# Row maxima of the second query tile in one instruction over two PSUM banks, with the order tables planned anew

## The chip, the cores and the metric

The kernel runs on one core of a Trainium2 chip. A core has five engines that run in parallel, each through its own in-order queue: TensorE (PE) for matmuls into PSUM, VectorE (DVE), ScalarE (ACT), GpSimd (POOL), and SyncE (SP), which issues most DMAs. The metric is the device time of one execution in microseconds (us); lower is better.

## The reference

Two layers run on `x` of 8 x 256 x 128. What the change touches is the attention of layer 0: 16 heads of width 8, once with ordinary queries and keys and once with six-component "lines" made from exterior products. Both softmaxes are causal.

```python
qkv = (x @ qkv_w + qkv_b).reshape(B, T, 3, H, dh)
std_logits = jnp.einsum('bhqd,bhkd->bhqk', q, k) * scale
w1 = (x_prev @ w1_write).reshape(B, T, H, 4)
write_lines = exterior(w1, w2)
read_lines = exterior(r1, r2)
J_write = jnp.einsum('bthi,ij->bthj', write_lines, _J6)
...
combined = (1.0 - gate) * std_out + gate * geo_out
return combined @ out_w + out_b
```

Around it stand, each with a residual and a layer norm: a feed-forward block with blockwise FP4 quantisation (layer 0), a Mamba block with a state scan over 256 steps, and a feed-forward block whose weights get a small data-dependent part ("LoRA", layer 1):

```python
x = _layernorm(x + _L0_attn_ref(...))
x = _layernorm(x + _L0_ffn_ref(x, w_gate, w_up, w_down))
x = _layernorm(x + _L1_attn_ref(...))   # the Mamba block
x = _layernorm(x + _L1_ffn_ref(...))    # the LoRA block
```

## The kernel before

**Turns.** The eight batch elements go through a software pipeline. Turn `k` (from -2 to 8) does `prep` for element k+2 (projections, splitting of the attention operands into bf16 parts), `core` for k+1 (logits, maxima, exponentials, weighting of the values), `norm`, `ffn`, `mamba` and `scan` for k, and `mamba_out` and `lora_ffn` for k-1. A turn has a front part (the chain norm, ffn, mamba of element k, with `prep`, the LoRA block and the first half of `core` between) and a scan part (the Mamba scan on DVE, with the second half of `core` on PE and ACT between).

**What sets the order.** Each engine's program is written out by `interleave`, which merges the streams of a turn by due times. The tables `PLAN` (turns 1 to 6) and `EDGE` (turns -1, 0, 7, 8) give one due time for each step of each stream (a step ends at a `yield`). The numbers are only an order: whatever stands earlier in an engine's queue runs first, and what stands behind a waiting instruction waits with it.

**The core of one element.** For each of two kinds of attention (a = 0, 1) the 16 heads go in four groups of four, g = 0 to 7 over both kinds. A group has three logit tiles of 128 x 512 (one PSUM bank of `ps_s` each): i = 0 is the first query tile against the first key tile for four heads, i = 1 and i = 2 are the second query tile against both key tiles for two heads each. That makes 24 tiles, n = 3g + i. PE writes tile n (a bf16 product of `stack` parts, on 72 rows, plus the causal mask through `ident_bf`) into bank n % 2, and DVE reduces it to the row maxima `mx` (L1062, counted by the semaphore `s_max`). After four groups PE transposes the maxima into bank 2 and DVE writes them as two bf16 parts, `mparts` (L1068, L1069, semaphore `m_sb`), which go through DRAM into `stack`. Then the second half of `core` computes the logits again, transposed, with the maximum subtracted (24 tiles over all three banks, waiting for the exponentials of ACT, L857), and PE weights the values (`weigh`). The third of these tiles waits for `m_sb`.

**Other steps that the prediction names.** `x3T,lmem` are the two halves of the first LoRA product (h1, 4 matmul passes each half); ACT takes them with Gelu (L937), and a second product waits for both. Then ACT loads its table again and copies the `prep` values (L837, L840, semaphore `hi_sb`), and POOL subtracts (L711) and, behind that, takes the roots of the layer norms (L728 and L729 in `root`). DVE's `y_out` (L987) is the layer norm of the LoRA block and waits for such a root; `z<-ps_f,x` (L1107) is the sum at the end of the feed-forward block. `xq<-x,rms_rstd` (L1134) is the Mamba input hx, PE transposes it and computes the convolution (`inWk`, 8 products) and the gate. `delta` (L1144) and `u` (L1148) start the scan part. In it, `hs` is the scan state (ring of 3), L1164 multiplies it with C, and PE adds it up in `ps_y` (8 steps j; step j of the scan waits for the sum of j-3). `zero_bf` matmuls ("warm" steps, two matmuls each) add zeros; they compute nothing.

## Time and profile before

| | |
|---|---|
| median of 3 runs (lowest, highest) | 853.65 us (847.95, 857.31) |
| the profiled execution: its own time, its span | 855.11 us, 853.3 us |
| busy, share of the span: PE, DVE, ACT, POOL | 81%, 72%, 48%, 46% |
| mean granted TensorE clock, share of full | 0.89 |
| L1062 (maxima) on DVE, 192 instructions | 127.1 us busy |

Times in the profile are from the start of the span. Busy shares are averages over stages with different limits. An instruction's idle time is put down to what it waited for last. The profile page ranks the costliest groups; the turn under study below is the one between about 380 and 472 us.

### The profile page before, as it was taken

How to read it: one execution, taken by the hardware profiler on the slowest of the kernel's cores; microseconds unless marked ns; L12 is line 12 of the kernel's file. 1: busy time of each engine (PE TensorE's matmuls, PEld its weight loads, DVE VectorE, ACT ScalarE, POOL GpSimd, SP SyncE). 2: the span in 40 equal slices, each digit the busy share in tenths (PEclk: the TensorE clock that was granted, in tenths of full speed). 3: DMA queues.
4: the chain of work that ended last, by engine and by line, in shares of the span. 5: the costliest groups of instructions: out<-in, count | busy, mean ns of one | idle time of the engine just before them, and what ended most of it. 6: DMA issues, size and time to landing. Idle time of an engine off the chain costs nothing. (4 is left out here: it accounts for less than half of the span.)

```text
span 853.3 us, 12511 instructions
## 1 busy us (share of the span) xinstructions
...
## 2 busy tenths in 40 slices
...
GB/s 133 86 97 37 116 22 23 127 166 27 2 153 128 89 0 84 144 138 0 48 136 178 7 1 151 151 59 1 102 145 117 2 16 154 46 2 6 146 53 7
DMA packets 40457, 66.10 MB, mean 77 GB/s; under 512 B 7282, under 2 KB 29635, under 8 KB 38083
## 3 DMA queue, kind: packets, MB, share of 16 engines
...
q10 hardware_dynamic: 2176, 1.05, 0.4%
...
q14 instruction: 18, 0.14, 0.1%
...
## 5 line engine op out<-in xcount | busy, mean ns | idle before, releaser
L765 POOL TENSOR_TENSOR shared<-u,bcrow 128x512 f32<-128x512 f32 x128 | 205.9, 1638 | 93.3 <-DVE u L1148 70.6
L1159 DVE TENSOR_TENSOR_SCAN shared<-ps_f,shared 128x512 f32<-128x512 f32 x128 | 150.9, 1209 | 26.0 <-PE ps_y L1198 9.9
L1198 PE MATMUL ps_s<-stack_mem 72*128 72x128 bf16 (+3 forms) x1024 | 148.4, 266 | 18.9 <-DVE mx L1062 12.6
L1062 DVE TENSOR_REDUCE mx<-ps_s 128x2 f32<-128x512 f32 (+1 forms) x192 | 127.1, 686 | 41.8 <-PE ps_s L1198 38.6
L1198 PE MATMUL ps_y<-shared,ident 128*128 128x512 f32 x256 | 124.0, 616 | 18.6 <-DVE shared L1164 18.5
L1198 PEld LDWEIGHTS ps_s<-stack_mem 74*128 74x128 bf16 (+1 forms) x1024 | 87.0, 106 | 83.7 <-DVE mx L1062 26.6
L926 ACT ACTIVATE ps_f<-delta,amat 128x255 f32<-128x255 f32 x256 | 110.6, 478 | 31.5 <-DVE shared L1159 17.9
L857 ACT ACTIVATE probs<-ps_s 128x512 f32<-128x512 f32 x192 | 106.5, 597 | 34.9 <-PE ps_s L1198 34.4
L1164 DVE TENSOR_TENSOR shared<-shared,bcrow 128x1024 f32<-128x1024 f32 x64 | 89.7, 1401 | 2.2
L1198 PE MATMUL ps_y<-zero_bf 128*128 128x512 bf16 x293 | 88.2, 416 | 1.4 <-DVE zero_bf L999 1.0
L728 POOL TENSOR_TENSOR rstd<-mv,cst 128x2 f32<-128x2 f32 x32 | 6.2, 195 | 175.0 <-DVE mv L979 175.0
L1198 PEld LDWEIGHTS ps_y<-shared,ident 128*128 128x128 f32 x256 | 45.6, 194 | 64.8 <-issue 37.4
L1198 PE MATMUL ps_s<-causalT,ident_bf 128*128 128x256 bf16 (+1 forms) x192 | 65.4, 341 | 4.7 <-DVE mparts L1069 4.7
L1198 PE MATMUL ps_s<-causal,ident_bf 128*128 128x256 bf16 (+1 forms) x192 | 64.2, 337 | 6.1 <-DVE mx L1062 4.3
L1198 PE MATMUL ps_v<-probs,vz 128*32 128x256 f32 (+1 forms) x1024 | 58.8, 350 | 1.4 <-ACT probs L857 1.0
L1198 PE MATMUL ps_n<-lmem 1*128 1x128 f32 (+1 forms) x224 | 35.1, 309 | 15.5 <-DMA lmem<-x 8.9
L1198 PEld LDWEIGHTS ps_v<-probs,vz 128*32 128x32 f32 x1024 | 27.8, 113 | 41.1 <-ACT probs L857 21.6
L1198 PEld LDWEIGHTS ps_y<-zero_bf 128*128 128x128 bf16 x293 | 30.6, 106 | 28.7 <-issue 9.5
L711 POOL TENSOR_TENSOR vals<-vals,parts 128x1024 f32<-128x1024 f32 x8 | 17.9, 2238 | 54.1 <-ACT parts L840 54.1
L1198 PEld LDWEIGHTS ps_n<-lmem 1*128 1x128 f32 (+1 forms) x224 | 30.6, 213 | 22.4 <-DMA lmem<-x 11.3
L1198 PE MATMUL ps_f<-wguT,xqT_mem 128*128 128x352 f32 x64 | 33.4, 660 | 0.5 <-ACT xqT_mem L873 0.5
L1198 PE MATMUL ps_f<-xqT_mem,inWk 128*128 128x256 f32 x128 | 32.8, 414 | 0.5 <-ACT xqT_mem L888 0.5
...
## 6 DMA issues: line engine op xcount, KB each, us to landing
...
```

The source lines that it names most:

```text
L711: G.tensor_tensor(rest1[:], vals[:], parts[:, 0], ALU.subtract).then_inc(rest1_sb, 1)
L728: chain(G.tensor_tensor(dst, v, eps.to_broadcast([P, TT]), ALU.add))
L765: G.tensor_tensor(bx[:, j % 2, c], u[:, c].unsqueeze(1).to_broadcast([P, 2, T]), bcrow[:, j % RING, 0], ALU.mult).then_inc(bx_sb, 1)
L857: A(probs[:, g % 3, (n % 3) * 512:(n % 3 + 1) * 512], ps_s[:, n % 3], ACT.Exp).then_inc(p_exp, 1)
L926: last = A(adisc[:, c, n, 1:T], delta[:, c, 1:T], ACT.Exp, scale=amat[:, c, 2 * j + n:2 * j + n + 1])
L1062: V.tensor_reduce(mx[:, a, min(i, 1), hd[0]:hd[-1] + 1:2], ps_s[:, n % 2].rearrange("p (h n) -> p h n", h=len(hd)), AX.X, ALU.max).then_in ...
L1159: V.tensor_tensor_scan(hs[:, j % HB, c].rearrange("p n t -> p (n t)"), ps_f[:, c, :], bx[:, j % 2, c].rearrange("p n t -> p (n t)"), 0.0, ...
L1164: V.tensor_tensor(hs[:, j % HB], hs[:, j % HB], bcrow[:, j % RING, 1].unsqueeze(1).to_broadcast([P, NC, 2, T]), ALU.mult).then_inc(hc_dve, 1)
L1198: return nc.tensor.matmul(o, lhsT, rhs, start=start, stop=stop, **kw)
```

## The change

The three banks of `ps_s` are used by tile now: i = 0 goes to bank 0, i = 1 and i = 2 to banks 1 and 2. DVE reduces tile 0 alone as before and tiles 1 and 2 of a group in one instruction over two banks, so there are 16 reductions of maxima per turn in place of 24. The waits follow: tile 0 of a group waits for the reduction of the previous tile 0, tiles 1 and 2 both wait for the previous two-bank reduction. Since bank 2 also holds the transposed maxima, tile 1 of group 4 (the first of the second kind) now waits for `m_sb`, that is for `mparts` of the first kind. And the order tables are written anew for several streams.

```diff
-                for n in range(24):
-                    a, e, i = n // 12, n // 3 % 4, n % 3
-                    yield
-                    hd = heads(e) if i == 0 else heads(e)[2 * i - 2:2 * i]
-                    dve.wait_ge(s_ps, f * 24 + n + 1)
-                    V.tensor_reduce(mx[:, a, min(i, 1), hd[0]:hd[-1] + 1:2], ps_s[:, n % 2].rearrange("p (h n) -> p h n", h=len(hd)), AX.X, ALU.max).then_inc(s_max, 1)
-                    if n % 12 == 11:
+                for g in range(8):
+                    a, hd = g // 4, heads(g % 4)
+                    for i in range(2):
+                        yield
+                        dve.wait_ge(s_ps, f * 24 + 3 * g + 2 * i + 1)
+                        if i == 0:
+                            tile = ps_s[:, 0].rearrange("p (h n) -> p h n", h=4)
+                        else:
+                            tile = ps_s[:, 1:3].rearrange("p b (h n) -> p (b h) n", h=2)
+                        V.tensor_reduce(mx[:, a, i, hd[0]:hd[-1] + 1:2], tile, AX.X, ALU.max).then_inc(s_max, 1)
+                    if g % 4 == 3:
...
-                    if n == 15:
+                    if g == 5:
...
-                    if n >= 2:
-                        pe.wait_ge(s_max, f * 24 + n - 1)
-                    bank = ps_s[:, n % 2]
+                    if g:
+                        pe.wait_ge(s_max, f * 16 + 2 * g - (1 if i == 0 else 0))
+                    if g == 4 and i:
+                        pe.wait_ge(m_sb, f * 2 + 1)
+                    bank = ps_s[:, i]
```

Of the tables for turns 1 to 6, four lines move steps on which the prediction rests. In SP's `rows` the third and fourth transfer of `bcrow` now follow the transfer of the maxima. In PE's `lora_ffn` both halves of h1 move back, and in DVE's `core` and `lora_ffn` the maxima and `y_out` move. In PE's `scan` the sums of j = 3 and j = 4 move forward. In PE's `warm` five steps move.

```diff
-        "rows": [68.7, 71.2, 71.5, 71.8, 72.1, 82.9, 87.2, 90.1, 93.8],
+        "rows": [68.7, 71.2, 71.5, 77.4, 77.7, 82.9, 87.2, 90.1, 93.8],
...
-        "lora_ffn": [13.5, 15.9, 21.6, 24, 26.1, 28],
+        "lora_ffn": [13.5, 15.9, 21.6, 27, 27.1, 28],
...
-        "scan": [68, 71.6, 75.6, 86.2, 89.7, 97.5, 102.5, 106.4],
+        "scan": [68, 71.6, 75.6, 81.3, 84.7, 97.5, 102.5, 106.4],
```

**Place 1: PE, front part of a turn, from the second half of the feed-forward's up product to the second LoRA product.** `ps_n<-x3T,lmem` are the two halves of h1, `ps_v<-ident,linesn` a transpose of `prep`, `ps_s` the tiles of group 3. Before:

```order
L1198 MATMUL ps_y<-zero_bf 128x512
L1198 MATMUL ps_n<-x3T,lmem 128x256 [waits weff]
L1198 MATMUL ps_n<-x3T,lmem 128x256
L1202 MATMUL ps_v<-ident,linesn 128x128 [waits vraw_sb,lin_n]
L1202 MATMUL ps_v<-ident,linesn 128x128 x3
...
L1198 MATMUL ps_s<-causal,ident_bf 128x2x128
L1198 MATMUL ps_n<-x3T,lmem 128x256 [waits h1_sb]
L1198 MATMUL ps_n<-x3T,lmem 128x256
```

Now:

```order
L1201 MATMUL ps_y<-zero_bf 128x512
L1205 MATMUL ps_v<-ident,linesn 128x128 [waits vraw_sb,lin_n]
L1205 MATMUL ps_v<-ident,linesn 128x128 x3
...
L1201 MATMUL ps_s<-causal,ident_bf 128x2x128
...
L1201 MATMUL ps_n<-x3T,lmem 128x256 [waits weff]
L1201 MATMUL ps_n<-x3T,lmem 128x256
L1201 MATMUL ps_n<-x3T,lmem 128x256 [waits h1_sb]
L1201 MATMUL ps_n<-x3T,lmem 128x256
```

The first half of h1 moved behind the transpose and two tiles; the second half, which waits for ACT's Gelu of the first (`h1_sb`), now stands directly behind it.

**Place 2: DVE, a little later, from the LoRA block's layer-norm statistics to `mparts` of the first kind.** `z<-ps_f,x` is the feed-forward sum. Before:

```order
L1062 TENSOR_REDUCE mx<-ps_s 128x2 [waits s_ps]
L1107 TENSOR_TENSOR z<-ps_f,x 128x256 [waits ffn_ps]
...
L987 TENSOR_SCALAR y_out<-z,mv,rstd 128x128 [waits lora_ln_rs,y_stored]
L987 TENSOR_SCALAR y_out<-z,mv,rstd 128x128
...
L1068 TENSOR_SCALAR mparts<-ps_s 16x256 [waits mT_ps]
L1069 SCALAR_TENSOR_TENSOR mparts<-ps_s,mparts 16x256 [waits dve_chain]
```

Now:

```order
L1065 TENSOR_REDUCE mx<-ps_s 128x4 [waits s_ps]
...
L986 TENSOR_SCALAR y_out<-z,mv,rstd 128x128 [waits lora_ln_rs,y_stored]
L986 TENSOR_SCALAR y_out<-z,mv,rstd 128x128
L1110 TENSOR_TENSOR z<-ps_f,x 128x256 [waits ffn_ps]
...
L1071 TENSOR_SCALAR mparts<-ps_s 16x256 [waits mT_ps]
L1072 SCALAR_TENSOR_TENSOR mparts<-ps_s,mparts 16x256 [waits dve_chain]
```

`y_out`, which waits for POOL's root of the LoRA norm, moved from behind the feed-forward sum to ahead of it.

**Place 3: PE, from the transposes of hx to the convolution `inWk`.** Before:

```order
L1202 MATMUL ps_f<-ident,xq 128x128 [waits hx_sb]
L1202 MATMUL ps_f<-ident,xq 128x128
L1198 MATMUL ps_y<-zero_bf 128x512 [waits yg_sb]
L1198 MATMUL ps_y<-zero_bf 128x512
...
L1198 MATMUL ps_s<-stack_mem 128x256 [waits s_max]
L1198 MATMUL ps_s<-stack_mem 128x256
L1198 MATMUL ps_s<-causal,ident_bf 128x2x128
L1198 MATMUL ps_f<-xqT_mem,inWk 128x256 [waits hxT_sb]
```

Now:

```order
L1205 MATMUL ps_f<-ident,xq 128x128
L1201 MATMUL ps_y<-zero_bf 128x512 [waits yg_sb]
L1201 MATMUL ps_y<-zero_bf 128x512
L1201 MATMUL ps_s<-stack_mem 128x256 [waits m_sb,s_max]
L1201 MATMUL ps_s<-stack_mem 128x256
L1201 MATMUL ps_s<-causal,ident_bf 128x2x128
L1201 MATMUL ps_y<-zero_bf 128x512 [waits yg_sb]
L1201 MATMUL ps_y<-zero_bf 128x512
L1201 MATMUL ps_y<-zero_bf 128x512 [waits yg_sb]
L1201 MATMUL ps_y<-zero_bf 128x512
L1201 MATMUL ps_f<-xqT_mem,inWk 128x256 [waits hxT_sb]
```

Two warm steps that stood ahead of the transposes of hx (three are left there of five) now stand between the last tile and the convolution.

## Rows read from the trace of the kernel before

**Rows 1.** Timeline, DVE, start of two turns (start us, us, engine line op, shapes, [idle before])
```profile
379.67 0.69 DVE L1170 TENSOR_TENSOR y<-ps_y,gsilu 128x512 f32<-128x512 f32 x1 [1.12 <-PE ps_y L1198]
...
471.82 0.69 DVE L1170 TENSOR_TENSOR y<-ps_y,gsilu 128x512 f32<-128x512 f32 x1 [1.12 <-PE ps_y L1198]
```

**Rows 2.** Groups of DVE by form: two reductions (busy us, mean ns | idle before)
```profile
L1062 DVE TENSOR_REDUCE mx<-ps_s 128x2 f32<-128x512 f32 x128 | 86.0, 685 | 17.4 <-PE ps_s L1198 15.5
...
L958 DVE TENSOR_REDUCE qamax<-fmem 128x44 f32<-128x704 f32 x8 | 7.1, 886 | 0.3
```

**Rows 3.** Timeline, DVE: the last maxima ahead of the up product's result
```profile
403.33 0.68 DVE L1062 TENSOR_REDUCE mx<-ps_s 128x2 f32<-128x512 f32 x1
404.11 0.89 DVE L1116 TENSOR_TENSOR fmem<-fmem,ps_f 128x704 f32<-128x704 f32 x1
```

**Rows 4.** Timeline, PE, around the two halves of h1
```profile
405.14 0.60 PE L1202 MATMUL ps_v<-ident,linesn 128*128 128x128 f32 x4
...
406.35 1.03 PE L1198 MATMUL ps_n<-x3T,lmem 128*128 128x256 f32 x4
```

**Rows 5.** Timeline, ACT: second Gelu pair, and the copy that releases POOL
```profile
407.41 0.84 ACT L937 ACTIVATE lmem<-ps_n,b1c 128x256 f32<-128x256 f32 x2 [1.23 <-PE ps_n L1198]
...
410.19 1.06 ACT L840 ACTIVATE parts<-vals 128x1024 bf16<-128x1024 f32 x1
```

**Rows 6.** Timeline, POOL: subtraction and the root of the LoRA norm
```profile
411.33 2.31 POOL L711 TENSOR_TENSOR vals<-vals,parts 128x1024 f32<-128x1024 f32 x1 [8.89 <-ACT parts L840]
414.06 0.20 POOL L728 TENSOR_TENSOR rstd<-mv,cst 128x2 f32<-128x2 f32 x1 [0.42 <-DVE mv L979]
414.34 0.70 POOL L729 TENSOR_TENSOR rstd<-rstd,cst 128x2 f32<-128x2 f32 x1
```

**Rows 7.** Timeline, DVE: from the feed-forward sum to the step ahead of hx
```profile
415.18 0.42 DVE L1107 TENSOR_TENSOR z<-ps_f,x 128x256 f32<-128x256 f32 x1 [0.38 <-PE ps_f L1198]
...
416.61 0.60 DVE L987 TENSOR_SCALAR y_out<-z,mv,rstd 128x128 f32<-128x128 f32 x2 [0.20 <-DVE mv L979]
...
417.91 0.14 DVE L1124 TENSOR_TENSOR rms<-rstd 128x2 f32<-128x2 f32 x1
```

**Rows 8.** Timeline, PE: warm steps, a tile and the convolution
```profile
415.97 2.32 PE L1198 MATMUL ps_y<-zero_bf 128*128 128x512 bf16 x10
...
420.17 0.59 PE L1198 MATMUL ps_y<-zero_bf 128*128 128x512 bf16 x2
420.60 0.38 PE L1198 MATMUL ps_s<-stack_mem 72*128 72x256 bf16 x2
...
420.93 3.62 PE L1198 MATMUL ps_f<-xqT_mem,inWk 128*128 128x256 f32 x16
```

**Rows 9.** Timeline, DVE: the last six maxima ahead of delta
```profile
430.00 3.98 DVE L1062 TENSOR_REDUCE mx<-ps_s 128x4 f32<-128x512 f32 x6 [1.04 <-PE ps_s L1198]
```

**Rows 10.** Timeline, PE, end of the scan part
```profile
458.94 0.39 PE L1198 MATMUL ps_s<-stack_mem 74*128 74x256 bf16 x2 [0.78 <-ACT probs L857]
...
460.67 1.94 PE L1198 MATMUL ps_y<-shared,ident 128*128 128x512 f32 x4
...
469.80 1.98 PE L1198 MATMUL ps_y<-shared,ident 128*128 128x512 f32 x4 [0.62 <-DVE shared L1164]
```

**Rows 11.** Timeline, DVE, end of the scan part: step j = 6
```profile
462.64 2.34 DVE L1159 TENSOR_TENSOR_SCAN shared<-ps_f,shared 128x512 f32<-128x512 f32 x2 [1.75 <-PE ps_y L1198]
```

**Rows 12.** Stretches of one turn: length, busy us of PE, PEld, DVE, ACT, POOL, then granted clock
```profile
390.50:393.90 3.40, 1.35 (x7) 0.45 (x5) 2.54 (x10) 0.78 (x2) 0.82 (x2) 1.00 0.01 2
393.90:400.80 6.90, 6.76 (x23) 4.64 (x24) 5.69 (x16) 3.46 (x7) 1.44 (x6) 0.51 0.00 0
...
415.20:431.50 16.30, 13.90 (x80) 8.80 (x78) 10.10 (x30) 7.07 (x14) 6.08 (x8) 1.00 0.27 78
431.50:434.90 3.40, 2.25 (x19) 1.24 (x17) 3.34 (x6) 1.23 (x3) 0.00 (x0) 1.00 0.95 323
434.90:441.70 6.80, 5.97 (x38) 2.92 (x36) 5.89 (x7) 4.86 (x11) 6.17 (x5) 0.50 0.33 130
```

More of the change, by code:

```diff
@@ L58 @@
         "prep": [10.4, 12.8, 14.9, 16.4, 17.9, 19.1, 22.9, 35, 42.3],
-        "core": [0.3, 68.9, 69.5, 70, 70.5, 71, 72.6, 72.7, 77.4, 78.6, 79.2, 81.5, 82.6, 84.4, 84.9, 85.5, 85.6,
-                 86.8, 87.4, 87.9, 90.5, 93.2, 93.3, 93.4, 93.8, 94.7, 96.6],
+        "core": [0.3, 68.9, 69.5, 70, 72.1, 72.6, 74.2, 74.3, 79, 80.2, 80.8, 83.1, 84.2, 86, 86.6, 87, 87.1, 88.4,
+                 89.1, 89.5, 92, 94.8, 94.9, 95, 95.4, 96.3, 98.2],
         "norm": [12.1],
@@ L64 @@
         "mamba": [47.1, 47.2, 62.2, 63.8],
-        "scan": [67.4, 69, 71.4, 75.5, 78, 79.3, 81.7, 82.9, 85.7, 86.5, 89, 92.1, 94.5, 94.6, 97.3, 98.5],
+        "scan": [67.4, 69, 71.4, 75.5, 78, 79.2, 81.7, 82.9, 85.7, 86.5, 89, 92.1, 94.5, 94.6, 97.3, 98.5],
     },
@@ L69 @@
         "norm": [4.6, 7.8, 11.5],
-        "core": [5.5, 6.1, 9, 9.6, 20.4, 21, 22.5, 24.3, 25.8, 34.1, 34.7, 36.7, 40.5, 45.6, 46.2, 47.4, 53.8, 55.5,
-                 56.2, 56.9, 57.5, 58.7, 59.3, 59.9, 60.6, 62.6],
-        "ffn": [15.8, 17.4, 17.8, 18.4, 19.4, 26, 28.8, 29.7, 30.8, 32.6, 38.5, 40.7],
+        "core": [5.5, 9, 9.6, 21, 22.5, 25.8, 34.1, 36.7, 40.5, 45.6, 47.4, 53.8, 56.2, 56.9, 58.7, 59.3, 60.6, 62.6],
+        "ffn": [15.8, 17.4, 18.8, 19.4, 19.5, 26, 28.8, 29.7, 30.8, 32.6, 38.5, 40.7],
         "prep": [22, 23.7],
-        "lora_ffn": [23.9, 25.5, 36.2, 38.9],
+        "lora_ffn": [23.5, 25, 35.8, 38.4],
         "mamba": [44.6, 50.8, 60.9],
@@ L87 @@
         "mamba_out": [6],
-        "lora_ffn": [13.5, 15.9, 21.6, 24, 26.1, 28],
+        "lora_ffn": [13.5, 15.9, 21.6, 27, 27.1, 28],
         "ffn": [16.6, 19.2, 22.5, 22.6, 30.4, 32.8],
         "mamba": [42.2, 45, 50.8, 51.9],
-        "scan": [68, 71.6, 75.6, 86.2, 89.7, 97.5, 102.5, 106.4],
+        "scan": [68, 71.6, 75.6, 81.3, 84.7, 97.5, 102.5, 106.4],
         "norm_std": [104.7],
-        "warm": [13.1, 21.1, 22.7, 38.3, 38.4, 39.5, 40.5, 41.5, 42.5, 53.5, 61.5, 77.8],
+        "warm": [13.1, 21.1, 22.7, 40.4, 40.5, 41.6, 42.6, 43.6, 44.6, 55.6, 63.6, 79.8],
     },
@@ L114 @@
             "setup": [0, 2.7, 6.3, 7.9, 12.9, 16.4, 19.6, 22.4, 25.7],
-            "core": [22.8, 24.1, 26.6, 28.1, 28.7, 29.7, 30.5, 31.2, 33.6, 34.2, 34.9, 35.5, 36.8, 37.6, 38.2, 38.9,
-                     39.6, 41.5, 42.3, 43, 43.6, 44.6, 45.4, 46.1, 47, 48.8],
+            "core": [22.8, 26.6, 28.1, 29.7, 30.5, 33.6, 34.2, 35.5, 36.8, 37.6, 38.9, 39.6, 42.3, 43, 44.6, 45.4,
+                     47, 48.8],
             "prep": [25.3, 27.2],
@@ L155 @@
         "dve": {
-            "core": [0, 0.6, 2.5, 3.2, 11.8, 12.5, 13.8, 16.8, 17.5, 31.3, 31.9, 34.8, 39, 43.1, 44.7, 45.3, 46.7,
-                     52.6, 53.3, 54, 55.2, 55.8, 56.5, 57.8, 58.4, 59.8],
+            "core": [0, 2.5, 3.2, 12.5, 13.8, 17.5, 31.3, 34.8, 39, 43.1, 45.3, 46.7, 53.3, 54, 55.8, 56.5, 58.4,
+                     59.8],
             "norm": [2.6, 6.1, 8.2],
-            "ffn": [8.4, 9.5, 9.9, 10.6, 11.5, 19.2, 22, 25.2, 28.6, 33.3, 37.8, 39.8],
+            "ffn": [8.4, 9.5, 9.9, 10.6, 11.5, 19.2, 22, 25.2, 28.6, 32.8, 37.4, 39.8],
             "prep": [13.1, 14.5],
-            "mamba": [43.7, 51.4, 60.6],
+            "mamba": [39.9, 50.4, 59.6],
             "scan": [64.4, 65.6, 66.9, 68.1, 69.3, 70.5, 71.7, 72.9, 74.2, 75.3, 76.5, 77.8, 79, 80.2, 81.5, 83.6,
@@ L166 @@
         "pe": {
-            "prep": [0, 1.1, 1.2, 5.1, 7.1, 8.2, 20.5],
+            "prep": [-9.8, -9.7, 1.1, 5.1, 7.1, 8.2, 20.5],
             "core": [0.5, 1, 3.5, 3.8, 6.4, 6.8, 14.3, 17.5, 18.1, 21.4, 21.9, 35.4, 39.1, 39.2, 40.6, 45.3, 47.1,
```

8 lines of the change are left out of this document (4 added, 4 removed).

## The prediction

> **What bounds the kernel now.** I read the timeline of DVE first, to find a turn. The same instruction starts at 379.67 and at 471.82 us [rows 1], so one turn of the loop takes 92.15 us. Six turns (1 to 6) run by the tables that the change rewrites most, so 1 us on a turn's path is 6 us in the result. Then I followed both parts of the turn through the timelines of all engines.
>
> In the **front part** one chain sets the time: the feed-forward block, its layer norm, the Mamba input hx, the convolution, delta and u. No engine is full there. The chain hops between DVE, POOL, ACT and PE, and the maxima and tiles of `core` stand between its links, in the same queues. So an instruction costs something if it stands ahead of a link that is ready, and nothing if it stands where the engine waits anyway. In the **scan part** PE's queue and DVE's scan hold each other: DVE stands 1.75 us ahead of step j = 6, for a sum that PE had queued behind other work [rows 11]; PE is idle 0.78 us for ACT and 0.62 us ahead of the last sum [rows 10].
>
> **The merged reduction.** One reduction of 512 elements takes 685 ns and one of 704 takes 886 [rows 2], so 1.05 ns an element and, for 1024, 1.22 us. In a burst six singles take 3.98 us [rows 9], 0.66 from start to start. A pair of them is 1.32, the merged one about 1.19: 0.13 us saved, eight times, 1.0 us of DVE time per turn. What of this lies on the path?
>
> - The burst ahead of delta (groups 6 and 7) is on it. Now tiles 1 and 2 of group 7 may only be written once the two-bank reduction of group 6 is over. PE needs 0.33 us a tile (420.60 to 420.93 in [rows 8]), so 0.66 for two, and some 0.2 to hand over (an estimate). DVE has one reduction of 0.66 to fill this. The burst is then 0.66 + 1.19 + 0.06 + 0.66 + 0.2 + 1.22 = 3.99 us against 3.98. The saving goes into a stall: 0.
> - Ahead of the product with the up projection, one single reduction (403.33) stands in front of the link at 404.11 [rows 3]; its partner ran earlier, while DVE waited. The merged one needs both and starts no earlier, so the link comes at 403.33 + 1.19 = 404.52: **0.4 us late**.
> - The other reductions stand where DVE waits: 0.
>
> **The LoRA half that moved (place 1).** The first half of h1 now stands behind a transpose and two tiles, which took from 405.14 to 406.35 [rows 4], so it comes 1.2 us later. The second half needs the first (1.03 us) and its Gelu (0.84 [rows 5]), about 2 us with the hand-overs, as far apart as the two were. So nearly all of it passes on; I take 1.15. ACT is in order, so the copy at 410.19 [rows 5] moves to 411.3 and POOL's subtraction from 411.33 [rows 6] to 412.5. It takes 2.31, so POOL is free at 414.8, and the root of the LoRA norm (0.28 to its second instruction, then 0.70 [rows 6]) is ready at 415.8.
>
> **y_out ahead of the feed-forward sum (place 2).** Before, `y_out` came after the sum and cost the chain little. Now DVE waits for that root, `y_out` takes 0.5 us, and the sum comes at 416.4 instead of 415.18 [rows 7]: **1.2 us late**, which contains the 0.4 from above. Part returns: the next link (417.91 [rows 7]) stood behind `y_out` and `mparts`, 2.7 us after the sum. With `y_out` gone it waits only for statistics and root, about 2.35 us. So hx is 0.8 us late. The price reaches from 0 (if the roots are in time after all) to 1.2.
>
> **The convolution (place 3).** Two warm steps stand directly ahead of it now. One takes from 420.17 to 420.60 [rows 8], 0.43 us. ACT's copy of hx is there before the single tile is through, so both count: **0.9 us**. Together the front part is 0.8 + 0.9 = 1.7 us longer, bounds 0.9 and 2.1.
>
> **The new wait for `m_sb`.** Tile 1 of group 4 waits for `mparts`, which DVE makes behind the late sum, at about 418.5. Queued behind it are that tile, three warm steps and the transposes of hx. The tile and the steps need 0.33 + 3 x 0.43 = 1.6 us, so PE is at hx by 420.1, and hx comes at about 420.7. The wait itself costs nothing. But PE stands from 416.2 to 418.5, where before ten zero matmuls began at 415.97 [rows 8].
>
> **The scan part.** The sums of j = 3 and j = 4 stand earlier in PE's queue, so DVE's stall of 1.75 us can go. Late next is PE itself: its work is the same, so it can only give up its idle time, 0.78 + 0.62 = 1.40 us, and with both sums gone from the end of its queue it must wait there for the last exponential. I take **1.0 us back** per turn, between 0 and 1.75. The exponentials on ACT are reordered around this; I cost that at nothing, because ACT waits several times there. So with the later transfers of `bcrow`: POOL, who reads them, runs ahead of DVE. If that cover is gone, the step j = 2 of the scan starts late by as much as its transfer lands late.
>
> **Turns -1, 0, 7, 8.** No lora step stands in turn -1 and turn 0, DVE's burst behaves as above, and in turn 7 and 8 there is no `core`. Each gets 0, with 1 us either way.
>
> **The sum.** 1.7 - 1.0 = 0.7 us per turn, six turns, **+4.2 us**: 859.3 us against the profiled execution's own 855.11, which stood 1.5 above the median; against the median 853.65 it is **857.9**. With the bounds (0.9 - 1.75 = -0.85 to 2.1 - 0 = +2.1 per turn) this case alone reaches from 848.5 to 866.
>
> **The rivals.**
>
> *A. TensorE's clock falls at the convolution (slower).* In this turn PE was busy 1.35 of 3.40 us and 2.25 of 3.40 us, and each time the next 6.8 to 6.9 us had a granted clock of 0.5 (1.2 GHz in place of 2.4), while from 415.20 to 431.50 it was busy 13.90 of 16.30 and the clock stayed at 1.00 [rows 12]. The new hole of 2.3 us with 0.6 more behind it makes the stretch ahead of the convolution look like the first two. A low stretch of 6.8 us over tile, warm steps and convolution costs at most half, 3.4; idle time absorbs some, I take 2.5 us a turn. It decides the result from three turns up: 865 to 873, at four turns 868. Against it: the hole is shorter than the gaps of the first stretch, and the clock also falls at 434.90, so a fall may only move. The Trainium skill (TensorE: Matmul & The Clock Gate, section "A second HAM failure mode: psum-queue depth-cycling") says that short idle times of TensorE between groups of matmuls, from cycling through PSUM banks, let the clock oscillate. By that rule this is the case to expect and the time would be 868; the 2.25 of 3.40 us ahead of the fall at 434.90 agrees with it.
>
> *B. The stall goes and the front holds (faster).* The roots are in time, DVE's idle slots swallow the rest, and the whole 1.75 us comes back: 6 x 1.75 = 10.5, 843 us. For it: it is a measured stall with a known cause. Against it: PE's idle time is less than this stall, and the two warm steps ahead of the convolution are plain in the order.
>
> *C. The edits cancel.* Front +1, scan -1: 853 to 855 us.
>
> **Chances.** Forecast 0.46, A 0.28, B 0.17, C 0.09. About 1% (8.5 us) is what a measurement of this kernel can tell from no change. Faster by more, below 845: most of B, 0.14. Slower by more, above 862: A and the upper tail of the forecast, 0.32. Within: 0.54. The likeliest case gives 858; the range over the cases, with no more than 2 in 10 left out, is 846 to 870; the forecast's own is 852 to 863.
>
> **What the changed profile would show.** A turn of 92.9 us between two `y` instructions. The feed-forward sum right behind `y_out`, and `y_out` idle for POOL's root; if it shows no wait, the 1.2 us is wrong. The link at 404.5 instead of 404.1 (in this turn's time). Two pairs of zero matmuls directly ahead of `inWk`, and PE idle some 2 us for `mparts` ahead of tile 1 of group 4. No wait of DVE for `ps_y` ahead of step 6. The granted clock between hx and delta: 1.00 for the forecast, 0.5 in several turns for A. What would make the forecast wrong above all is that clock, and a scan part that gives back nothing or everything.

## The result, and the profile after

Both kernels ran ten times on one chip. The changed kernel takes 862.22 us (median, 858.33 to 864.79), the kernel before 853.73 us: ratio 1.0103, 95% interval 1.0066 to 1.014. It is 1% slower. The profiled execution took 863.64 us, with a span of 861.8 us (before: 855.11 and 853.3), so the two traces differ by 8.5 us, as the medians do. Each trace is of one execution, and the ten executions of the changed kernel spread over 6.5 us, so what recurs in every turn is firm below, and a few us in one place may belong to that execution alone. Of `u_warm` below, two executions took 877 us and four 855.3 to 860.8; its profile is one of the two, its ratio is of the four.

**One turn.** Timeline of DVE in the changed kernel: the two instructions that answer to [rows 1], and the links between them.

```profile
383.24 0.69 DVE L1173 TENSOR_TENSOR y<-ps_y,gsilu 128x512 f32<-128x512 f32 x1 [0.87 <-PE ps_y L1201]
...
405.56 0.75 DVE L1187 SCALAR_TENSOR_TENSOR lmem<-ps_n,lscale,w2T 128x512 f32<-128x512 f32 x1 [2.14 <-PE ps_n L1201]
406.23 1.22 DVE L1065 TENSOR_REDUCE mx<-ps_s 128x4 f32<-128x1024 f32 x1
407.36 0.88 DVE L1119 TENSOR_TENSOR fmem<-fmem,ps_f 128x704 f32<-128x704 f32 x1
...
418.59 0.60 DVE L986 TENSOR_SCALAR y_out<-z,mv,rstd 128x128 f32<-128x128 f32 x2 [0.61 <-POOL rstd L728]
419.10 0.42 DVE L1110 TENSOR_TENSOR z<-ps_f,x 128x256 f32<-128x256 f32 x1
...
421.40 0.16 DVE L1127 TENSOR_TENSOR rms<-rstd 128x2 f32<-128x2 f32 x1
...
422.87 0.48 DVE L1137 TENSOR_SCALAR xq<-x,rms_rstd 128x128 f32<-128x128 f32 x2 [0.59 <-POOL rms_rstd L728]
...
434.37 2.48 DVE L1065 TENSOR_REDUCE mx<-ps_s 128x4 f32<-128x512 f32 x3
437.18 1.23 DVE L1065 TENSOR_REDUCE mx<-ps_s 128x4 f32<-128x1024 f32 x1 [0.33 <-PE ps_s L1201]
438.32 0.68 DVE L1147 SCALAR_TENSOR_TENSOR delta<-fmem 128x512 f32<-128x512 f32 x1
...
465.18 2.32 DVE L1162 TENSOR_TENSOR_SCAN shared<-ps_f,shared 128x512 f32<-128x512 f32 x2
...
475.26 0.69 DVE L1173 TENSOR_TENSOR y<-ps_y,gsilu 128x512 f32<-128x512 f32 x1 [0.87 <-PE ps_y L1201]
```

This turn (turn 3) takes 92.02 us, before 92.15. `y_out` waits 0.61 us for POOL's root, as forecast, and the sum stands right behind it. Step j = 6 of the scan (465.18) has no wait, where [rows 11] had 1.75 us. Part of that went elsewhere: two of the eight multiplications with C (L1167, L1164 before) take 1.77 and 1.98 us in this turn, where the same two took 1.36 and 1.23. The runs do not show why.

By form, DVE's two kinds of maxima in the changed kernel (busy us, mean ns, idle before):

```profile
L1065 DVE TENSOR_REDUCE mx<-ps_s 128x4 f32<-128x1024 f32 x64 | 78.2, 1222 | 24.9 <-PE ps_s L1201 24.3
L1065 DVE TENSOR_REDUCE mx<-ps_s 128x4 f32<-128x512 f32 x64 | 44.0, 687 | 20.0 <-PE ps_s L1201 18.8
```

The merged reduction takes 1222 ns, the estimate was 1.22 us. All maxima together fall from 127.1 us busy to 120.8, and DVE's idle time ahead of them rises from 41.8 us (17.4 + 24.4) to 44.9.

PE of the changed kernel in the same turn: both halves of h1, the tile that waits for `mparts`, the convolution, and the end of the scan part.

```profile
408.38 1.03 PE L1201 MATMUL ps_n<-x3T,lmem 128*128 128x256 f32 x4
410.34 1.13 PE L1201 MATMUL ps_n<-x3T,lmem 128*128 128x256 f32 x4 [0.93 <-ACT lmem L936]
...
421.37 0.39 PE L1201 MATMUL ps_s<-stack_mem 72*128 72x256 bf16 x2 [2.33 <-DVE mparts L1072]
...
424.44 1.02 PE L1201 MATMUL ps_y<-zero_bf 128*128 128x512 bf16 x4
425.31 3.62 PE L1201 MATMUL ps_f<-xqT_mem,inWk 128*128 128x256 f32 x16
...
468.38 0.86 PE L1201 MATMUL ps_v<-probs,vz 128*32 128x256 f32 x16 [0.69 <-ACT probs L856]
469.17 3.70 PE L1201 MATMUL ps_y<-shared,ident 128*128 128x512 f32 x8
```

**Where the 8.5 us are.** Instants of each turn, from the start of `y` of the turn, read from the DVE and PE timelines of both traces. The last column is the change over turns 1 to 6.

| stretch | turn 3, before | turn 3, after | all six, change | forecast x 6 |
|---|---|---|---|---|
| `y` to the second LoRA weight (`w2T`) | 22.99 | 22.32 | -1.2 | 0 |
| from there to hx | 16.70 | 17.31 | +2.3 | +4.8 |
| hx to convolution | 1.57 | 2.44 | +5.2 | +5.4 |
| convolution to delta | 12.97 | 13.01 | +0.3 | 0 |
| delta to the next `y` (scan part) | 37.92 | 36.94 | -3.1 | -6.0 |
| six turns | | | +3.5 | +4.2 |

The first `y` comes 2.2 us later (198.86 for 196.65), and turns 7 and 8 are 2.8 us longer. 2.2 + 3.5 + 2.8 = 8.5 us.

**The clock.** Stretches of the changed kernel's turn: length, busy us of PE, PEld, DVE, ACT, POOL, granted clock, as in [rows 12]. A low stretch is one with a granted clock of about 0.5.

```profile
396.10:402.90 6.80, 5.36 (x20) 3.97 (x20) 6.30 (x16) 2.54 (x5) 0.00 (x0) 0.50 0.01 1
413.10:416.50 3.40, 2.55 (x22) 2.06 (x20) 3.30 (x8) 2.84 (x5) 1.08 (x1) 1.00 0.00 0
416.50:419.90 3.40, 2.27 (x19) 1.92 (x19) 2.63 (x8) 1.28 (x2) 1.90 (x3) 1.00 0.00 0
419.90:423.30 3.40, 1.80 (x9) 0.80 (x9) 2.48 (x12) 0.00 (x0) 1.80 (x4) 1.00 0.02 5
437.10:440.50 3.40, 1.09 (x9) 0.68 (x8) 3.25 (x5) 1.46 (x4) 0.53 (x1) 1.00 0.44 177
440.50:443.90 3.40, 3.34 (x27) 1.91 (x27) 2.53 (x4) 3.04 (x8) 3.40 (x4) 0.50 0.23 53
```

In turns 1 to 5 of this profile no low stretch lies between the up product and delta, and in turn 6 only one over the down product (3.4 us at 32.0 us of the turn; the kernel before has one there in turns 1 and 6). Over the hole and the convolution the clock stayed at 1.00 in all six: rival A did not happen in this execution. But two things moved. In turn 3 the low stretch ahead of the up product begins 12.9 us into the turn in place of 14.2, and the one behind delta is 3.4 us long in place of 6.8 (in the turn at 567.39 it is 6.8, and that scan part took 38.30 us, not 36.94).

So there are two readings of the scan part's 1.0 us. **Theory S**: the earlier sums gave it. **Theory K**: the shorter low stretch gave it. And three questions: what does the merged reduction do without the new tables, what did the front tables cost, and what cost 5 us at the edges?

### The profile page after: what moved, and what is told of

Its sections match the earlier page's. It is cut to its first block and busy times, and to the rows that moved or that the text cites. A ratio compares the mean times of both kernels' runs of the same rounds, so it can differ in the third digit from the quotient of the medians.

```text
span 861.8 us, 12481 instructions
## 1 busy us (share of the span) xinstructions
PE 686.0 (80%) x4232; PEld 413.3 (48%) x4232; DVE 610.3 (71%) x999; ACT 411.0 (48%) x816; POOL 379.2 (44%) x473
## 5 line engine op out<-in xcount | busy, mean ns | idle before, releaser
L764 POOL TENSOR_TENSOR shared<-u,bcrow 128x512 f32<-128x512 f32 x128 | 199.8, 1594 | 107.7 <-DVE u L1151 75.4
L1065 DVE TENSOR_REDUCE mx<-ps_s 128x4 f32<-128x512 f32 (+1 forms) x128 | 120.8, 955 | 44.9 <-PE ps_s L1201 43.1
L1201 PEld LDWEIGHTS ps_s<-stack_mem 74*128 74x128 bf16 (+1 forms) x1024 | 90.0, 105 | 84.6 <-issue 29.4
L1167 DVE TENSOR_TENSOR shared<-shared,bcrow 128x1024 f32<-128x1024 f32 x64 | 95.0, 1485 | 2.2
L1201 PE MATMUL ps_y<-zero_bf 128*128 128x512 bf16 x293 | 86.3, 406 | 1.4 <-DVE zero_bf L998 1.0
L1201 PEld LDWEIGHTS ps_y<-shared,ident 128*128 128x128 f32 x256 | 44.7, 192 | 58.2 <-issue 35.4
L1201 PE MATMUL ps_n<-lmem 1*128 1x128 f32 (+1 forms) x224 | 37.9, 326 | 15.9 <-DMA lmem<-x 9.4
L1201 PEld LDWEIGHTS ps_n<-lmem 1*128 1x128 f32 (+1 forms) x224 | 33.0, 228 | 23.3 <-DMA lmem<-x 11.7
```

Source lines behind the costliest of these rows:

```text
L764: G.tensor_tensor(bx[:, j % 2, c], u[:, c].unsqueeze(1).to_broadcast([P, 2, T]), bcrow[:, j % RING, 0], ALU.mult).then_inc(bx_sb, 1)
L1065: V.tensor_reduce(mx[:, a, i, hd[0]:hd[-1] + 1:2], tile, AX.X, ALU.max).then_inc(s_max, 1)
L1167: V.tensor_tensor(hs[:, j % HB], hs[:, j % HB], bcrow[:, j % RING, 1].unsqueeze(1).to_broadcast([P, NC, 2, T]), ALU.mult).then_inc(hc_dve, 1)
L1201: return nc.tensor.matmul(o, lhsT, rhs, start=start, stop=stop, **kw)
```

## The experiments

Every ratio is against the kernel before, on the same chip; the runs below come from three chips, so compare ratios and not times between rows. The changed kernel itself has 1.0103. "Turn" is the mean of turns 1 to 5 of the profiled execution; the kernel before has 91.9 us, the changed one 92.4.

| kernel | us | ratio [95%] | turn |
|---|---|---|---|
| u_sums: old place of the sums | 892.0 | 1.0442 [1.0404, 1.048] | 98.0 |
| u_warm: old warm steps | 859.3 | 1.0037 [0.9993, 1.0081] | 95.6 |
| u_edge: old tables of turns 0 and 7 | 862.2 | 1.009 [1.0055, 1.0125] | 93.2 |
| merge_only: all tables old | 874.8 | 1.0242 [1.0207, 1.0277] | 95.6 |
| a_mid: changed, four warm steps in the hole, none ahead of the convolution | 861.0 | 1.0052 [1.0011, 1.0092] | 92.5 |
| a_early: changed, seven more steps ahead of the up product | 858.3 | 1.0045 [1.001, 1.008] | 92.4 |
| a_all: a_mid and a_early, four more behind the last maxima | 856.8 | 1.0022 [0.998, 1.0064] | 91.6 |
| b_sums: before, sums moved | 859.6 | 1.0038 [1.0006, 1.0071] | 92.1 |
| merge_fill: merge_only, four warm steps in the hole | 863.0 | 1.011 [1.007, 1.0151] | 93.3 |
| b_fill: before, seven more steps | 848.1 | 0.9941 [0.9919, 0.9962] | 90.5 |
| a_best: changed, a_mid and a_early and two more | 849.5 | 0.9957 [0.9934, 0.9979] | 90.8 |
| u_front: old places of h1 and y_out | 875.0 | 1.0243 [1.0198, 1.0287] | 95.6 |

### The scan part: u_sums and b_sums

```diff
-        "scan": [68, 71.6, 75.6, 81.3, 84.7, 97.5, 102.5, 106.4],
+        "scan": [68, 71.6, 75.6, 86.2, 89.7, 97.5, 102.5, 106.4],
```

> The changed kernel with one part undone: in turns 1 to 6 the sums of j = 3 and j = 4 stand where they stood before the change. Theory S (the earlier sums gave back the 1.0 us that the changed kernel's scan part is shorter, 36.94 in place of 37.92 us from delta to y): the wait of 1.7 us for ps_y ahead of step j = 6 is back, the scan part is 37.9 us again in each of the six turns, and the time is 862.2 + 6 = 868 us. Theory K (the scan part is shorter because the stretch at half clock behind delta is 3.4 us long in place of 6.8; the turn of the kernel before that had 3.4 us there, the one at 196.65, had 36.98 us too, with the wait for ps_y in it): the wait is back, at 1.2 us, but the scan part stays at 37.0 us where the low stretch is 3.4 us, and the time is 862 +- 1 us.

Both theories missed: the scan part takes 40.9 to 42.4 us, and each turn has one more low stretch, of 3.4 or 6.8 us, late in the scan part. DVE ahead of step j = 6 in this kernel, and PE ahead of the sum it waits for:

```profile
482.80 2.34 DVE L1162 TENSOR_TENSOR_SCAN shared<-ps_f,shared 128x512 f32<-128x512 f32 x2 [4.68 <-PE ps_y L1201]
```
```profile
477.59 0.43 PE L1201 MATMUL ps_s<-stack_mem 74*128 74x256 bf16 x2 [2.13 <-ACT probs L856]
...
480.43 2.34 PE L1201 MATMUL ps_y<-shared,ident 128*128 128x512 f32 x4
```

In its old place the sum stands behind tiles that wait for exponentials, and the change made these later in ACT's table (from the fifth on, by 1.5 to 1.7 in due time). I had costed that reordering at nothing. The sums and the exponentials are one change: half of it costs 30 us. (That ACT's table is the other half is argued from this wait; ACT's table alone was not tried, and how much of the 30 us the added low stretches make is open.)

The other way round, the sums moved in the kernel before:

> The kernel before, with one part of the change alone: in turns 1 to 6 the sums of j = 3 and j = 4 stand earlier in PE's queue. Theory S (that gives the scan part its 1.0 us): the wait of 1.75 us ahead of step j = 6 is gone, the scan part 36.9 us in place of 37.9 us, 854 - 5 = 849 us. Theory K (the end is set by PE's and ACT's queue of tiles and exponentials, and the 1.0 us came from a shorter low stretch): the wait is gone but others take its place, scan part 37.9 us with a low stretch of 6.8 us and 37.0 with one of 3.4, 854 us. Rival (an earlier sum delays the exponentials behind it, since the order on ACT is the old one): 855 to 860 us.

The wait for `ps_y` is gone, and another stands in its place. DVE at step j = 6 and PE at its last wait for ACT, turn at 377.35:

```profile
460.37 2.34 DVE L1159 TENSOR_TENSOR_SCAN shared<-ps_f,shared 128x512 f32<-128x512 f32 x2 [2.42 <-ACT ps_f L926]
```
```profile
461.61 0.86 PE L1198 MATMUL ps_v<-probs,vz 128*32 128x256 f32 x16 [1.43 <-ACT probs L857]
```

With a low stretch of 6.8 us its scan parts take 38.7 us (before: 37.6 to 38.0), without one 36.6; the kernel as a whole is 0.4% slower. The earlier sums alone bring nothing. Theory S, in which they suffice, is refuted.

For theory K speak the scan parts of all profiles in which sums and exponentials stand in matching places, old or new. With a low stretch of 3.4 us behind delta: before 36.98; b_fill 37.00 and 37.04, merge_fill 36.99 and 37.08 (old order); after 36.94 to 37.12 (new order). With 6.8 us: before 37.61 to 38.02, merge_fill 37.88 to 38.17, after 38.30, a_best 37.94 to 38.21. The order makes no difference that shows; turns with 3.4 us more at half clock take 1.0 us longer. That is a comparison of turns, and no run changed the clock behind delta alone. (Not all fit: merge_only has 37.3 to 37.4 with 6.8 us, a_mid 37.2 in one such turn, 37.0 in the one with 10.2 us and 38.1 in one with 3.4 us, and a_all two of 38.3 with 3.4 us that begin at 62 to 65 us of the turn. So the place counts too.)

### The merged reduction alone, and the hole: merge_only, u_front, merge_fill

In merge_only the code of the change stands with every order table as in the kernel before; only DVE's `core` keeps its 18 entries, since a merged reduction stands where the later of its two stood.

> The merged maxima with their banks and waits alone: all order tables as before the change, apart from the maxima of tiles 1 and 2, which stand where the later of the two stood. Theory M: the link at the up product 0.4 us late in each turn, and tile 1 of group 4, which waits for mparts, stands ahead of five warm steps (0.33 + 5 x 0.43 us behind 418.4), so that the transposes of hx are 0.6 us late; scan part as before: +1.0 us x 6 turns, 860 us. Rival 1 (waits swallow both): 854 us. Rival 2 (a hole in PE moves the low clock stretch ahead of the up product, as in the changed kernel where that gave 0.67 us a turn back): +0.3 a turn, 856 us.

Too low by 15 us. In turn 3 hx is 1.2 us late, the convolution 3.5, and each of turns 1 to 5 has a low stretch of 3.4 us at 40.7 to 40.8 us, between hx and the convolution. Here rival A is real. u_front is the changed kernel with three lines of turns 1 to 6 undone:

```diff
-        "lora_ffn": [13.5, 15.9, 21.6, 27, 27.1, 28],
+        "lora_ffn": [13.5, 15.9, 21.6, 24, 26.1, 28],
-        "ffn": [15.8, 17.4, 18.8, 19.4, 19.5, 26, 28.8,
+        "ffn": [15.8, 17.4, 17.8, 18.4, 19.4, 26, 28.8,
-        "lora_ffn": [23.5, 25, 35.8, 38.4],
+        "lora_ffn": [23.9, 25.5, 36.2, 38.9],
```

> The changed kernel with the steps of the LoRA block back in their old places in turns 1 to 6: both halves of h1 earlier on PE, y_out behind the feed-forward sum on DVE, and two quantisation steps of DVE as before. Theory Y (y_out's wait for POOL's root delays the sum): the sum at 35.2 in place of 35.86 us of the turn, but mparts then stands behind y_out again and hx 0.3 us earlier, at 39.3: 862.2 - 6 x 0.3 = 860 us. Rival 1 (mparts behind y_out keeps PE's tile and the warm steps behind it late, the transposes of hx wait): hx on PE no earlier, 862 us. Rival 2 (the down product falls into a low stretch as in the kernel with the merged maxima alone, whose places for h1 are these): +1.3 to 3.5 us a turn, 870 to 880 us.

Its rival 2 came true: by the ratios (1.0243 for 1.0103) these three lines together are worth some 12 us, a gain where the forecast had a cost of 0.8 us a turn. Stretches of u_front ahead of and over the down product and the convolution:

```profile
418.40:421.80 3.40, 1.38 (x11) 0.90 (x9) 3.30 (x8) 1.69 (x3) 2.26 (x1) 1.00 0.00 0
421.80:425.20 3.40, 3.12 (x14) 2.93 (x15) 1.51 (x4) 1.29 (x2) 1.25 (x3) 0.52 0.00 0
425.20:428.60 3.40, 1.39 (x12) 0.86 (x10) 3.06 (x13) 0.00 (x0) 1.27 (x4) 0.98 0.00 0
428.60:432.00 3.40, 3.40 (x12) 1.60 (x10) 1.10 (x4) 1.01 (x2) 0.59 (x1) 0.52 0.30 87
```

PE is busy 1.38 of 3.40 us and the clock falls over the down product; then 1.39 of 3.40 (the wait for `mparts`), and it falls at the convolution. In the changed kernel the LoRA products run later, in the hole ahead of the down product (410.34 to 414.45), and PE is busy 2.55 of 3.40 us from 413.10 to 416.50 (the same place of the turn, row above), and 2.27 and 1.80 in the next two: no fall. So the move of h1 fills a hole. That it is h1, of the three lines, is argued from these rows; no run moved it alone. The kernel before, with its h1 in the old place, has the fall over the down product too, in turns 1 and 6.

The changed tables do not keep the second fall away for good. u_edge (below) has the changed kernel's tables in turns 1 to 6, and in its turns 1 and 5 the clock falls at the convolution, which starts 3.6 us behind hx in place of 2.4. Turn 1 of u_edge, ahead of the fall and behind it:

```profile
231.40:234.80 3.40, 1.20 (x12) 0.85 (x11) 2.55 (x10) 0.79 (x1) 1.40 (x3) 1.00 0.00 0
234.80:238.20 3.40, 3.27 (x10) 1.48 (x11) 1.99 (x8) 0.00 (x0) 1.03 (x3) 0.50 0.09 25
```

The hole ahead of tile 1 of group 4 is 2.33 us there as in the changed kernel. So rival A is most likely open to the changed kernel as well, in some turns of some executions, and its one profile has none of them. The Trainium skill (TensorE: Matmul & The Clock Gate, section "A second HAM failure mode: psum-queue depth-cycling") says that short idle times between groups of matmuls make the clock go up and down. In merge_only and u_front the traces agree, with 95.6 us a turn, and so do two turns of u_edge; at this place of the changed kernel's profile they don't.

merge_fill puts zeros into the hole of merge_only: four warm steps ahead of tile 1 of group 4, three behind it in place of five.

```diff
-        "warm": [13.1, 21.1, 22.7, 38.3, 38.4, 39.5, 40.5, 41.5, 42.5, 53.5, 61.5, 77.8],
+        "warm": [13.1, 21.1, 22.7, 36, 36.1, 36.2, 36.3, 38.3, 40.5, 41.5, 42.5, 53.5, 61.5, 77.8],
```

> The kernel with the merged maxima alone and the old order tables, whose turns take 95.5 us (conv at 44.7 us of a turn, low stretches of 3.4 us at 34 and 41 us): now four warm steps stand ahead of tile 1 of group 4, in the hole in which it waits for mparts, and three behind it in place of five. Theory W (the wait for mparts costs by what is queued behind it, five warm steps, and by the hole): hx reaches PE on time, conv at 42.4, turn 93.3 us, 875 - 6 x 2.2 = 862 us. Theory C (the clock falls at the down product, ahead of this hole, for another reason, and the fill cannot help that): the low stretch at 34 us stays with its 1.25 us in the down product, conv at 43.9, 870 us. If the low stretch at 41 us goes and the one at 34 stays, both carry a part.

Stretches of merge_fill, the same places:

```profile
412.90:416.30 3.40, 1.37 (x10) 1.06 (x11) 3.17 (x9) 1.50 (x4) 2.71 (x2) 1.00 0.00 0
416.30:419.70 3.40, 3.40 (x16) 2.91 (x17) 1.70 (x4) 1.03 (x1) 0.79 (x2) 0.50 0.00 0
419.70:423.10 3.40, 3.31 (x21) 1.60 (x20) 2.57 (x12) 0.00 (x0) 1.82 (x4) 1.00 0.02 5
423.10:426.50 3.40, 3.34 (x19) 2.36 (x18) 2.30 (x4) 1.67 (x2) 0.54 (x2) 1.00 0.44 125
```

The first fall stays (in three turns of five), the second is gone, and the convolution starts 42.4 us into the turn in place of 44.7 (turn 3; 41.8 to 42.7 in turns 1 to 5). So the new wait for `m_sb` costs 2.2 us a turn with the old tables, by its hole and by the steps queued behind it; the run does not part the two. Both parts of the expectation hold: 863.0 us, for the 862 it named.

Both kernels, and u_warm, show one more cost of the old line of warm steps. A step (433.94 in merge_fill) stands there between two tiles of the burst ahead of delta, DVE waits for the tile behind it, and the way from convolution to delta is 13.45 us; with the new line it is 13.02. DVE in merge_fill:

```profile
434.90 1.82 DVE L1065 TENSOR_REDUCE mx<-ps_s 128x4 f32<-128x1024 f32 x2 [0.40 <-PE ps_s L1201]
```

### The warm steps: u_warm and a_mid

u_warm has the old line of warm steps, five ahead of hx and none directly ahead of the convolution (all nine entries from the fourth on, not five, 2.0 to 2.1 less in due time: 38.3, 38.4, 39.5, 40.5, 41.5, 42.5, 53.5, 61.5, 77.8).

> The changed kernel with the warm steps of turns 1 to 6 back at their old due times, so five stand ahead of the transposes of hx and none between the last tile and the convolution. Theory W (the two steps are on the path for their whole length): delta comes 0.87 us earlier in each turn, less what the five steps cost behind the wait for mparts (tile 0.33, five steps 2.15 us from 421.37, so the transposes at 423.85 in place of 423.41): net 0.4 us a turn, 860 us. Rival 1 (they are off the path): no change, 862 us. Rival 2 (the burst moves against the clock, the low stretch behind delta grows to 6.8 us again as it did in the turn at 567.39, where the scan part was 38.30 us in place of 36.98): 0.4 us gained and up to 1.3 lost a turn, 862 to 868 us.

The ratio, 1.0037 for 1.0103 (the intervals overlap), fits Theory W. In the profile, which is not of an execution that the ratio stands for, each of turns 1 to 5 has a low stretch of 3.4 us at 38.6 to 38.8 us, and the convolution starts at 43.9 to 44.2 us: rival A is possible with this kernel. Turn 6 has no such stretch; there the convolution starts 1.96 us behind hx in place of 2.44, and the burst ahead of delta takes 0.43 of this back. So the two steps ahead of the convolution are on the path, and they may guard the clock. a_mid separates this: four steps in the hole ahead of the tile, none ahead of the convolution.

```diff
-        "warm": [13.1, 21.1, 22.7, 40.4, 40.5, 41.6, 42.6, 43.6, 44.6, 55.6, 63.6, 79.8],
+        "warm": [13.1, 21.1, 22.7, 36, 36.1, 36.2, 36.3, 40.4, 40.5, 41.6, 42.6, 55.6, 63.6, 79.8],
```

> The changed kernel, turns 1 to 6, with warm steps placed otherwise around the wait for mparts: four new ones ahead of tile 1 of group 4 (where PE was idle 2.33 us), and the two between the last tile and the convolution left out. Theory C (the hole is what lets the clock fall at the convolution in some runs, and the two steps behind hx cost their length): conv starts 0.87 us earlier in the turn (41.2 in place of 42.07), delta at 54.2, no low stretch between 30 and 45 us of a turn: 862.2 - 5 = 857 us. Rival 1 (the two steps behind hx kept the clock up through the convolution): a low stretch of 3.4 us at 38 to 41 us of a turn, as in the slow profile of the run with the old warm steps, conv at 44: 862 + 11 = 873 us. Rival 2 (another stretch reacts): 862 us.

Convolution 1.58 us behind hx as before the change, and no low stretch at 38 us in any of six turns, as theory C said. The 0.87 us gained are the two steps, and filling the hole gave nothing beside them: the wait itself had cost nothing here. The low stretch behind delta takes 6.8 us in three turns and 10.2 in one (it now begins at 51.6 to 57.6 us), which eats part of the 5 us: 1.0052 for 1.0103 (other runs, another chip; the intervals overlap).

### The edges: u_edge

```diff
-            "norm": [0, 4.8, 4.9],
+            "norm": [0, 2.2, 3.6],
-            "ffn": [..., 28.6, 32.8, 37.4, 39.8],
+            "ffn": [..., 28.6, 33.3, 37.8, 39.8],
-            "mamba": [39.9, 50.4, 59.6],
+            "mamba": [43.7, 51.4, 60.6],
-            "prep": [-9.8, -9.7, 1.1, 5.1, 7.1, 8.2, 20.5],
+            "prep": [0, 1.1, 1.2, 5.1, 7.1, 8.2, 20.5],
-            "scan": [69.7, 73.3, 76.9, 82.6, 85.5,
+            "scan": [69.7, 73.3, 76.9, 80.6, 85.5,
```

> The changed kernel with the tables of turns 0 and 7 as before the change (PE's prep and scan, DVE's ffn and mamba in turn 0, PE's norm in turn 7); the merged maxima stay. Theory E (PE's norm steps, moved behind a warm step, make turn 7 longer by 2.7 us, y to y 88.22 in place of 85.49): turn 7 is 85.5 us again. Turn 0's scan part, 39.44 us against 36.78, goes back if the order made it: then both give 5 us, 857 us. Rival (the low stretch of 13.7 us in turn 7, in place of 6.8, and those of turn 0 come from where the preceding turns end against the clock): at most one of the two edges changes, 860 to 862 us.

Turn 0's scan part is 36.94 us, turn 7 takes 85.31, both as before the change; but three of turns 1 to 6 lost more to the clock (turns 1 and 5 at the convolution, as shown above, turn 6 behind delta), and the time stays, with a ratio of 1.009 for 1.0103. Turn 0 is settled over all profiles: with the new tables of turn 0 its scan part takes 38.9 to 39.7 us (eight kernels), with the old ones 36.8 to 36.9 (six). Even so the first `y` comes at 192.7 to 199.7 us with the new tables and at 193.2 to 197.3 with the old ones, so one trace says little of what this costs. One wait of the changed kernel that the old order does not have, at step j = 1:

```profile
168.45 2.50 DVE L1162 TENSOR_TENSOR_SCAN shared<-ps_f,shared 128x512 f32<-128x512 f32 x2 [1.44 <-ACT ps_f L925]
```

Which of the lines of turn 0 does it was not tried. Turn 7 is another matter: it takes 85.2 to 86.0 us in the seven profiles in which its low stretch near 10 us is 6.8 us long, and 87.7 to 89.8 in the seven in which it is 10.2 to 17.1, with the old place of the norm steps on both sides. Theory E is right for turn 0 and wrong for turn 7.

### Zeros ahead of the up product: a_early, a_all, b_fill, a_best

The low stretch ahead of the up product is in every turn of both kernels. Warm steps fill the holes in front of it. a_early adds seven at one place of the table of the changed kernel:

```diff
-        "warm": [13.1, 21.1, ...
+        "warm": [13.1, 13.2, 13.3, 13.4, 13.42, 14, 14.1, 14.2, 21.1, ...
```

> The changed kernel with seven more warm steps in turns 1 to 6, in the two places ahead of the up product where PE stood idle: four where it waits for DVE's x (2.18 us), three behind the transposes of x (1.44 us). Theory H (the holes let the clock fall; the low stretch of 6.8 us at 13 us of a turn costs the link at w2 some 1.4 us): no low stretch there, w2 at 21.0 in place of 22.35 us of the turn, all behind it as much earlier: 862.2 - 6 x 1.4 = 854 us. Rival 1 (the fall is not made by these holes): low stretch as before, 862 us. Rival 2 (the fall moves to a later place, the down product or the convolution, as in the kernel with the merged maxima alone, where turns took 95.5 us): 862 to 875 us.

In three of turns 1 to 6 w2 comes at 18.2 to 20.7 us, in three there is a low stretch of 3.4 us at 17 us and w2 stays at 22.3. In two turns the clock falls at 37 to 38 us and the convolution is 3.7 us behind hx, which is rival 2. Each of the three had a part.

a_all has the steps of a_early and of a_mid, and four late ones:

```diff
+        "warm": [13.1, ..., 22.7, 36, ..., 42.6, 55.6, 57, 57.1, 59, 59.1, 63.6, 79.8],
```

> Both changes to the warm steps above, and four more steps where PE waits behind the last maxima and for the second mparts (1.32 and 1.05 us at 54 to 57 us of a turn). Theory H: no low stretch in turns 1 to 6 at all; w2 1.4 us earlier, conv 0.87, and the scan part 1.0 us shorter than 36.98 (a stretch of 6.8 in place of 3.4 cost it 1.3 us in the turn at 567.39): 3.3 us a turn, 842 us. Rival 1 (the clock falls elsewhere): a low stretch in another place, 850 to 862 us. Rival 2 (the added steps delay the work behind them as much as the clock gives back): 862 us.

One turn has no low stretch at all and takes 89.93 us; its scan part is 37.00. So taking the last 3.4 us of low clock away gives the scan part nothing. In three turns the clock falls at 51 us instead, in two at 62 to 65. Theory H was wrong by this part, and 856.8 us lies in the range of rival 1.

b_fill is the kernel before with seven more steps, in its own holes:

```diff
-        "warm": [13.1, 21.1, 22.7, ...
+        "warm": [7.5, 7.55, 13.1, 13.2, 14, 14.1, 14.2, 16, 21.1, 22.7, ...
```

> The kernel before, with seven more warm steps in turns 1 to 6 in the places ahead of the up product where PE stood idle (two in the wait of 1.34 us for maxima, one in 0.75 us, three in 1.43 us, one behind the first LoRA products). Theory H (TensorE at full clock through the up product): no low stretch between 14 and 21 us of a turn, w2 at 20.7 in place of 22.99 or 22.37 us, 854.5 - 6 x 1.9 = 843 us. Rival 1 (the clock falls later, at 17 us, as in two turns out of five with the steps added to the changed kernel): w2 at 22.3, 852 us. Rival 2 (the gain lets another stretch fall, at the convolution): 855 us or more.

Stretches of b_fill, of the turn at 377.60, that answer to the first two of [rows 12]:

```profile
388.40:391.80 3.40, 3.09 (x15) 1.24 (x13) 2.53 (x10) 0.78 (x2) 0.85 (x3) 1.00 0.01 2
391.80:398.60 6.80, 5.86 (x36) 3.78 (x36) 6.20 (x16) 3.42 (x7) 1.32 (x6) 1.00 0.00 0
```

w2 comes at 21.44 us in all of turns 1 to 5, in place of 22.23 to 22.99: 848.1 us, 0.6% faster than before, 5 us less gain than expected. a_best has the steps of a_early and of a_mid, one more at 16 and one at 51.5:

> The changed kernel with the warm steps ahead of the up product (eight, one of them behind the first LoRA products, where 0.59 us of idle time was left and the clock still fell at 17 us in some turns), with four ahead of tile 1 of group 4 and none between the last tile and the convolution, and one ahead of the product for delta (0.67 us of idle time). Theory H: w2 at 20.7, conv at 39.9, delta at 53, a turn of 90 us as the one turn without a low stretch had in the kernel with all warm steps: 862.2 - 6 x 2.1 = 850 us, and up to 3 less at the edges. Rival (the clock falls somewhere in most turns whatever holes are filled): 856 us, as that kernel.

849.5 us. It beats the kernel before by 0.4% and the changed one by 12.7 us. b_fill and a_best are 0.2% apart, within their intervals. With such steps in both kernels (seven more in one, eleven more net in the other), the merged maxima with their tables make no difference that these runs can tell from none.

## Why the prediction was right, and where it was not

The forecast was 858 us for the kernel, against 862.2, and "within 1%" the likeliest; the measured 1.0% lies on that edge. The six turns came out at +3.5 us for +4.2, and this is in part luck: the front gave 6.6 us for 10.2, the scan part gave back 3.1 for 6.0, and the two misses cancel.

- **Burst ahead of delta, 0**: right. The burst takes 4.04 us (434.37 to 438.41) with a wait of 0.33 for PE ahead of its last reduction, for 3.98 in [rows 9], and the way from convolution to delta is 13.01 us for 12.97. The 0.2 us to hand over had no row behind it. And the prediction did not see that a warm step had to leave the burst for this: where it stayed, 0.43 us were lost (u_warm, merge_only, merge_fill).
- **Link +0.4**: right, 1.80 us from `w2T` to the link for 1.45: +0.35. But the link as a whole comes 24.1 us into the turn, 0.3 earlier than before and not 0.4 later, by the up product.
- **h1 +1.15**: right. From `w2T` to POOL's subtraction 9.86 us for 8.67: +1.19.
- **y_out and the sum, 1.2 late**: 1.02, and hx 0.61 late for 0.8. But the sign of the move as a whole was wrong. It was costed against turn 3 of the old front, where the clock does not fall; with the merged reduction in place, undoing it costs some 12 us (u_front).
- **Convolution +0.9**: right, 0.87, and the holes of 2.33 us for `mparts` and the two pairs of zeros are there.
- **The `m_sb` wait costs nothing**: true in this profile (a_mid fills the hole and gains the 0.87 us of the two steps, no more). With the old tables it is 2.2 us a turn (merge_only against merge_fill), and in two turns of u_edge, with the new ones, the clock falls behind it, at 1.2 us each.
- **Scan part 1.0 back**: the size holds for three of the six turns (0.8 to 1.0; 0.6 in one, none in two), the step is wrong. It rested on the sums; b_sums shows that alone these give nothing, and turns with equal low stretches behind delta take about equal time in the old order and the new. That PE "must wait there for the last exponential" was true (0.69 us at 468.38). What was put at nothing, the order on ACT, is most likely the other half of the move: alone the earlier sums leave DVE waiting for ACT (b_sums), and under ACT's new order the old sums lose 30 us (u_sums). The cover for `bcrow` held: step j = 2 has no wait.
- **Up product, not in the sum**: -0.67 us in turn 3. PE's idle time there is one hole of 2.18 us now (1.34 and 0.75 before) and the clock fell and rose 1.4 us earlier in the turn, which is the probable reason. Over six turns -1.2.
- **Turns -1, 0, 7, 8 at 0 with 1 us each**: the term that failed in size, in this trace. +2.2 up to the first `y` (the scan part of turn 0 alone +2.7, its tables) and +2.8 in turns 7 and 8 (a longer low stretch, which comes and goes with either table). That the time would be 857 us without them is not so: u_edge had both back and took 862.2.

Rival A named the mechanism that decides these kernels, at the right place: it is what the merged reduction does in every turn without the new tables, and in some turns of u_edge with them, though in none of the changed kernel's profile. Its forecast of 6.8 us low and 2.5 us a turn was 3.4 us low and 2.3 us from hx to the convolution where it came (merge_only). Rival B's whole 1.75 us was not to be had. Which turn of the changed kernel gets a long low stretch behind delta (one of six in this profile) stays open.
